# Attention and a routed expert layer: moments kept later, scores waited for by chunk, planning over more tiles, results loaded ahead of z

## What is computed

```
n  = layernorm(x)
q  = relu(n @ Wq + bq); k = relu(ctx @ Wk + bk); v = relu(ctx @ Wv + bv)
x1 = x + relu((relu(q @ k.T) / sqrt(512) + mask) @ v)
z  = layernorm(x1)
topv, topi = top_k(z @ gate_w, 2);  w = softmax(topv)
y_e = (silu(z @ Wu[e]) * (z @ Wv[e])) @ Wo[e]
out = x1 + sum over the two chosen e of w_e * y_e
```

## Time and profile before

| | |
|---|---|
| median of three runs | 429.07 us |
| the profiled execution, span | 429.35 us, 427.6 us |
| TensorE's granted clock, mean | 0.991 of full speed |
| TensorE busy | 404.1 us, 94% |
| VectorE busy | 344.8 us, 81% |
| ScalarE busy | 267.5 us, 63% |
| chain that ended last | TensorE 55%, VectorE 23%, ScalarE 7% |

### The profile page before, as it was taken

The page is one execution under the profiler, slowest core; times in us unless marked ns, Lnnn a source line. Parts: engine busy times, 40 slices in busy tenths (PEclk is TensorE's granted clock), DMA queues, the critical chain, the costliest instruction groups (busy, mean ns, idle before and its releaser), DMA issues.

```text
span 427.6 us, 10469 instructions
## 1 busy us (share of the span) xinstructions
PE 404.1 (94%) x3063; PEld 359.5 (84%) x3063; DVE 344.8 (81%) x1126; ACT 267.5 (63%) x581; POOL 194.5 (45%) x231
## 2 busy tenths in 40 slices
PE   8999999999999999998989889999999998999990
PEld 5698988998889988888778778888999997899970
DVE  2679899999999999999767878778887767888760
ACT  1677877778778777776667656666666443344430
POOL 2011135556655555554546743333333154666641
PEclk9999999999999999999999999999999999999996
DMA  8812235877767677544766868779964689999830
GB/s 288 266 64 70 92 100 202 286 270 255 250 219 240 230 258 260 191 152 159 236 236 194 302 190 278 246 232 304 280 205 104 221 271 366 387 368 400 320 137 36
DMA packets 53622, 97.98 MB, mean 229 GB/s; under 512 B 8384, under 2 KB 19136, under 8 KB 53440
## 3 DMA queue, kind: packets, MB, share of 16 engines
q1 hardware_dynamic: 41648, 63.21, 46.4%
q0 software_dynamic: 11920, 34.10, 21.0%
HBM read 54.15 MB, written 50.80 MB: 245 GB/s over the span
## 4 chain that ended last, share of the span: by engine, by line
PE 55%; DVE 23%; ACT 7%; issue 5%; DMA 3%; SPq 2%; POOL 1%; POOLq 0%; DVEq 0%; ACTq 0%
PE psQ L1531 9%; PE psQ L1532 9%; PE psQ L1533 9%; PE psT L1527 6%; DVE st L1138 4%; DVE x L1127 4%; PE psS L1531 3%; DVE qpT L955 2%; PE psQ L1527 2%; PE psO L1531 2%; PE psZ L1533 2%; PE psZ L1531 2%; PE psO L1532 2%; PE psO L1533 2%; PE psZ L1532 2%
## 5 line engine op out<-in xcount | busy, mean ns | idle before, releaser
L955 DVE TENSOR_TENSOR qT<-psT,qT 128x512 fp32r<-128x512 f32 x103 | 69.4, 688 | 25.5 <-ACT qT L751 25.4
L1531 PE MATMUL psQ<-wuv,qT 128*128 x284 | 86.4, 304 | 0.0
L657 POOL DMA_INDIRECT z_dram<-zb x64 | 70.9, 1108 | 31.3 <-issue 15.3
L1532 PE MATMUL psQ<-wuv,qT 128*128 x284 | 80.2, 283 | 0.0
L1533 PE MATMUL psQ<-wuv,qT 128*128 x284 | 80.1, 282 | 0.0
L1531 PE MATMUL psQ<-qT,wq 128*128 128x256 f32 x256 | 75.1, 294 | 0.0
L1533 PE MATMUL psQ<-qT,wq 128*128 128x256 f32 x256 | 72.4, 283 | 0.0
L1532 PE MATMUL psQ<-qT,wq 128*128 128x256 f32 x256 | 72.4, 283 | 0.0
L751 ACT ACTIVATE qT<-psT 128x512 fp32r<-128x512 f32 x103 | 59.5, 594 | 15.2 <-PE psT L1527 15.2
L1531 PEld LDWEIGHTS psQ<-wuv,qT 128*128 128x128 f32 x284 | 53.7, 189 | 3.0
L1532 PEld LDWEIGHTS psQ<-wuv,qT 128*128 128x128 f32 x284 | 54.0, 190 | 0.0
(11 more groups left out here) (325 smaller groups left out, 1050.5 us busy)
## 6 DMA issues: line engine op xcount, KB each, us to landing
wq<-z_dram SPq DMA_DIRECT2D x42, 264.0 KB, 4.0
xin<-in_x_dram SPq DMA_DIRECT2D x11, 512.0 KB, 4.6
z_dram<-spare SPq DMA_DIRECT2D x17, 264.0 KB, 4.6
qpT<-z_dram SPq DMA_DIRECT2D x17, 264.0 KB, 3.8
acc_dram<-spare SPq DMA_DIRECT2D x17, 256.0 KB, 4.8
...
```

The source lines that it names most:

```text
L657: pool.indirect_dma_start(out=z_dram, out_offset=bass.IndirectOffsetOnAxis(ap=z_of(b)[:, t, ROW_COL + k:ROW_COL + k + 1].bitcast(U32), axi ...
L955: nc.vector.tensor_tensor(o, a, b, ALU.subtract).then_inc(s, 1)
L1531: pe.matmul(o, w[LO], a[HI], start=first, stop=False)
L1532: pe.matmul(o, w[HI], a[LO], start=False, stop=False)
```

## The change

1. `norm_x` leaves VectorE's steps; ScalarE normalises both halves of the next block, one after the other (only the first block keeps it).
2. `keep_stats` moves behind `turned_x`.
3. Scores wait for chunk c's low part ahead of chunk c, not for all four ahead of the first.
4. `turn_logits` is two transposes over the strips; a VectorE reduce (`folded`) adds them into SBUF, and max and max_index read there. The next gate matmuls wait for the reduce. `pick` goes.
5. The plan begins at tile 8 instead of 7 and ends at tile 22 instead of 20; `turn_sched` stands after tiles 10 and 20. `know_pads` moves from tile 7 to 11, and with it SP's copies of the tails go behind `load_z`.
6. From tile 50 on, SP asks for first results ahead of `load_z(t)`, and for 44 and 45 both at tile 50, so that up to tile 56 the results run one ahead of where they were.
7. Two waits are written otherwise and hold the same numbers (15 both times).

```diff
...
@@ -268,7 +268,7 @@
         ps_held = psG[0:1, BT + P:BT + 2 * P]
         ps_key = [psS, psG, psQ[0], psQ[1]]
         ps_log = psG[:, 0:BT]
-        ps_logit = psG[:, BT:BT + TPB * E].rearrange("p (t e) -> p t e", e=E)
+        ps_strips = psG[:, 0:BT].rearrange("p (t c s) -> p t s c", t=TPB, s=STRIP)[:, :, 0:E, :]
         ps_pos = psG[:, BT + 32:BT + 32 + TPB * K * E].rearrange("p (t k e) -> p t k e", k=K, e=E)
         ps_tot = psG[:, BT + 96:BT + 96 + K * E].rearrange("p (k e) -> p k e", e=E)
         psST = [psQ[i][:, 2 * R:2 * R + P] for i in range(2)]
@@ -569,17 +570,12 @@
 
 
             bulk = FIRST_B + RING - 1
-            accs = {bulk - 1: [FIRST_B + LATE, FIRST_B, FIRST_B + 1, FIRST_B + LATE + 1, FIRST_B + LATE + 2]}
-            todo = list(range(FIRST_B + LATE + 3, TILES))
+            todo = [FIRST_B + LATE, *range(FIRST_B, FIRST_B + LATE), *range(FIRST_B + LATE + 1, TILES)]
+            accs = {bulk - 1: [todo.pop(0) for _ in range(5)]}
             for t in range(bulk, TILES):
-                accs[t] = [todo.pop(0) for _ in range(2 if t in (bulk + 4, bulk + 6) else 1)]
+                accs[t] = [todo.pop(0) for _ in range(2 if t in (bulk, bulk + 4) else 1)]
             accs[TILES] = todo
             for t in range(TILES):
-                if EARLY <= t < EARLY + E:
-                    if t == EARLY:
-                        sp.wait_ge(pads_known, 2)
-                        sp.wait_ge(head_stored, 16 * E)
-                    copy_tail(t - EARLY)
                 if FULL + 2 <= t < FULL + 2 + E:
                     fill_acc(t - FULL - 2)
                 if bulk - HELD // 2 <= t < bulk:
@@ -593,10 +589,16 @@
                         sp.wait_ge(res_stored[a % RING], 16 * (rounds(a) + 1))
                     for a in accs[t - 1]:
                         load_acc(a)
-                load_z(t)
                 if t >= bulk:
                     for a in accs[t]:
                         load_acc(a)
+                load_z(t)
+                if EARLY <= t < EARLY + E:
+                    if t == EARLY:
+                        sp.wait_ge(pads_known, 2)
+                        sp.wait_ge(head_stored, 16 * E)
+                    copy_tail(t - EARLY)
+                if t >= bulk:
                     for h in range(HELD):
                         if held_wanted(h) == t:
                             load_held(h)
@@ -769,7 +771,7 @@
 
                 ge(act, nmr1_ready, b.n + 1)
                 nc.scalar.activation(xn[:, t, 0:D], x_of(b)[:, t, :], ACT.Identity, bias=nmr1[:, t:t + 1],
-                                     scale=rstd1[:, t:t + 1]).then_inc(xn1_ready, 1)
+                                     scale=rstd1[:, t:t + 1]).then_inc((xn0_ready, xn1_ready)[t], 1)
 
             def turned_x(b, t):
                 ge(act, xn_turned, 2 * b.n + t + 1)
@@ -877,6 +879,7 @@
                 if not nxt.real:
                     nc.scalar.activation(warm[:, :], minus_half[:, 0:1], ACT.Silu).then_inc(warmed, 1)
                 else:
+                    norm1(nxt, 0)
                     norm1(nxt, 1)
                 queries(2)
                 queries(3)
...
@@ -1172,13 +1173,15 @@
 
                 def values(self):
                     ge(dve, logit_turned, self.b.n + 1)
+                    nc.vector.tensor_reduce(logits[:, :, :], ps_strips, AX.X, ALU.add).then_inc(folded, 1)
+                    ge(dve, folded, self.b.n + 1)
                     for t in range(TPB):
-                        nc.vector.max(top_v[:, t, :], ps_logit[:, t, :]).then_inc(route, 1)
+                        nc.vector.max(top_v[:, t, :], logits[:, t, :]).then_inc(route, 1)
 
                 def indices(self):
                     ge(dve, route, self.n + 2)
                     for t in range(TPB):
-                        nc.vector.max_index(top_i[:, t, :], top_v[:, t, :], ps_logit[:, t, :]).then_inc(route, 1)
+                        nc.vector.max_index(top_i[:, t, :], top_v[:, t, :], logits[:, t, :]).then_inc(route, 1)
 
                 def gaps(self):
                     ge(dve, egap_ready, self.b.n)
@@ -1365,7 +1368,6 @@
                     add_attention(prv, 1)
                 if nxt.real:
                     norm1.shift()
-                    norm_x(nxt)
                 if third.real:
                     put.ranks()
                     put.picked()
@@ -1389,12 +1391,13 @@
                 low(3)
                 if prv.real:
                     norm2.shift()
-                    keep_stats(prv)
                 for t in range(TPB):
                     if nxt.real:
                         turned_x(nxt, t)
                     else:
                         turned_g(t)
+                if prv.real:
+                    keep_stats(prv)
                 if ends_early:
                     plan_ends(0)
                     plan_rows(0)
@@ -1483,35 +1486,37 @@
                     put.rows()
                     put.write()
                     Weigh(last).all()
+                if t == 8:
                     dve.wait_ge(place, PLACE_STEPS * NB)
+                    plan_lengths(1)
+                if t == 9:
+                    plan_ends(1)
+                if t == 10:
+                    plan_rows(1)
+                if t == 11:
+                    keep_sched(1)
                     know_pads()
-                    plan_lengths(1)
-                if t == 8:
-                    plan_ends(1)
-                if t == 9:
-                    plan_rows(1)
-                if t == 10:
-                    keep_sched(1)
                     plan_used(1)
-                if t == 11:
+                if t == 12:
                     lists_sizes()
-                if t == 12:
+                if t == 13:
                     lists_rests()
-                if t == 13:
-                    lists_ends(range(0, 3))
                 if t == 14:
-                    lists_ends(range(3, 5))
                     lists_starts()
                 if t == 15:
+                    lists_ends(range(0, 3))
+                if t == 16:
+                    lists_ends(range(3, 5))
                     lists_skips()
-                if t == 16:
+                if t == 17:
                     lists_rows()
-                if t == 17:
+                if t == 18:
                     lists_heads()
-                if t == 18:
+                if t == 19:
                     lists_cuts()
-                if t == 20:
+                if t == 21:
                     keep_sched(2)
+                if t == 22:
                     keep_kinds()
                 if is_held(t + 1):
                     own_of(t + 1)
@@ -1601,10 +1606,10 @@
 
             def scores(b):
                 g = b.n // NB_G
-                ge(pe, qp_lo, 4 * b.n + 4)
                 if b.n == 0:
                     pe.wait_ge(k_lo, DC)
                 for c in range(DC):
+                    ge(pe, qp_lo, 4 * b.n + c + 1)
                     ins = three(psS[:, 0:BT], [kpT[:, h, c, g * KEYS:(g + 1) * KEYS] for h in range(2)],
                                 [qpT[:, h, c, :] for h in range(2)], c == 0, c == DC - 1)
                 ins.then_inc(s_done, 1)
@@ -1621,6 +1626,7 @@
                 if b.n == 0:
                     pe.wait_ge(w_loaded["small"], 32)
                 ge(pe, zT_ready, 2 * b.n + 2)
+                ge(pe, folded, b.n)
                 ge(pe, place, PLACE_STEPS * (b.n - 1) + 3)
                 for c in range(DC):
                     ins = pe.matmul(ps_log[c * STRIP:(c + 1) * STRIP, :], gw[:, c, :], zT[:, c, :], start=True, stop=True,
@@ -1639,16 +1645,14 @@
 
             def turn_logits(b):
                 ge(pe, logT_ready, b.n + 1)
-                if b.n == 0:
-                    pe.wait_ge(conv_ready, 7)
                 for t in range(TPB):
-                    ins = pe.matmul(ps_logit[:, t, :], logT[:, t * P:(t + 1) * P], pick[:, :], start=True, stop=True)
+                    ins = turn(ps_log[:, t * P:(t + 1) * P], logT[:, t * P:(t + 1) * P])
                 ins.then_inc(logit_turned, 1)
 
             def turn_sched(g):
                 pe.wait_ge(plan, PLANNED[g])
                 if g == 0:
-                    pe.wait_ge(lg_ready, NB - 1)
+                    pe.wait_ge(lg_ready, EARLY_NB + 3)
                 if g == 1:
                     pe.wait_ge(place, PLACE_STEPS * NB)
                 if g > 1:
@@ -1725,7 +1729,7 @@
                     turn_g(1)
                 if old.real:
                     gates(old)
-                if not nxt.real:
+                if b.n == EARLY_NB + 3:
                     pe.wait_ge(sched_ready, 2)
                 scores(b)
                 if old.real:
@@ -1770,9 +1774,9 @@
                     turn_logits(last)
                 if t == 6:
                     ranks(last)
-                if t == 9:
+                if t == 10:
                     turn_sched(1)
-                if t == 19:
+                if t == 20:
                     turn_sched(2)
```

7 lines of the change are left out of this document (3 added, 4 removed).

## The result

The change makes the kernel about 1% slower: five runs took 431.57, 433.84, 434.09, 434.64 and 435.52 us, median 434.09, against 429.07 for five runs of the kernel before. The ratio is 1.0107 (95%: 1.0061 to 1.0153). 427.8 had been forecast, within 424.3 to 431.3, and a time over 433.4 had been given a chance of 0.07. The profiled execution is the shortest of the five, 431.57 us with a span of 429.8, 2.2 us over that of before; the others are 2.3 to 4 us longer still, at a mean granted clock of 0.984 to 0.988 in place of 0.991. So there are two things to find: 2.2 us in the trace, and most of the rest beside it.

A forecast was written before the change was run, and what follows sets the result against it. It took TensorE (busy 94%) and, where it sets the pace, VectorE (81%) as bounds. Terms -1.0 + 0.8 - 0.3 - 1.1 + 2.1 - 1.8 = -1.3 gave 428.05, and 427.8 for the median, range 424.3 to 431.3.

The forecast's parts named there:

- first steps: Attention steps 0 to 2: the bare ScalarE detour delays the turned parts and next projection; +0.8 us (0 to 1.2).
- attention, twelve steady steps: Steps 3 to 14: VectorE's round decides, 0.09 us less a step counted; -1.0 us (-3.0 to +2.4).
- end of the stage: Last attention step: earlier scores -0.5, moved instructions ahead of the low parts +0.2; -0.3 us (-0.7 to +0.2).
- plan, up to tile 23: Plan tiles: links spread over more tiles, tile 7 relieved of 0.9; -1.1 us (-1.6 to -0.4).
- results from tile 48: Tile 46's first result asked for earlier, 0.65 there, about 1.1 from held rows and tiles behind; -1.8 us (-0.6 to -2.6).
- Tile 25's rows: At `turn_g(25)`: schedule written one tile later, rows late, TensorE waits two microseconds; +2.1 us (0.8 to 3.2).
- 0.53 us "before the scores": Attention step: TensorE's wait for low(3) ahead of the scores, said to go with scores by chunk.
- rival 2: Results from tile 48: held rows take the result's place entirely, only 0.6 of 1.8 got; 429.0; chance 0.13.
- Rival 1: low(2) in each step: the ScalarE detour is dearer than its rows say; 432.0; chance 0.2.
- rival 3: Tile 25's rows not late, or little, as the issue follows the schedule faster than 0.90; 425.7; chance 0.1.
- rival 4: Attention steps: VectorE's round falls without the 0.4 us at low(2), 0.3 more a step; 424.0; chance 0.1.

The follow-up runs named there:

- before_again: The kernel before, unedited, run once more for its trace; 428.42 us.
- tails_pool: The changed kernel with the eight copies of tails issued by GpSimd ahead of its stores instead of by SP; ratio 1.0128 to the kernel before.
- plan_only: The kernel before with point 5 alone (plan over more tiles, copies of tails behind `load_z`); ratio 1.0078, +3.3 us.
- after_again: The changed kernel, unedited, run again; ratio 1.0114 to the kernel before in its group.
- attn_only: The kernel before with the attention edits alone (points 1 to 4); ratio 1.0044, +1.9 us.
- after_fixed_2: Second run of the changed kernel with tails ahead of the rows, pads at tile 8, last schedule at tile 20; 428.84 us against 429.47, ratio 0.9986.
- bulk: The kernel before with point 6 alone (the new order of results); ratio 0.9984, -0.7 us.

## Why the prediction was wrong, point by point

The measured column compares the profiled executions of the two kernels, 427.6 and 429.8 us long, by the same marks in both.

| term | forecast | measured | from |
|---|---|---|---|
| start, to nmr of step 0 | none | -0.6 | 25.34 (24.96 in `before_again`) to 24.75 |
| first steps | +0.8 | +0.95 | nmr of step 0 to step 2, 20.85 to 21.80 |
| attention, twelve steady steps | -1.0 | -0.4 | nmr of step 2 to step 14, 142.10 to 141.68 |
| end of the stage | -0.3 | -0.3 | nmr of step 14 to the turn at 211.77, 23.83 to 23.54 |
| plan, up to tile 23 | -1.1 | -0.9 | 66.19 to 65.25 (66.39 in `before_again`) |
| tiles 24 and 25 | +2.1 | +3.9 | three turns, 8.5 to 12.4 |
| results from tile 48 | -1.8 | -0.45 | turn of tile 26 to that of tile 70, 122.26 to 121.81 |
| fall of the clock | none | +1.4 to +1.7 | where it falls, other traces |

The rows but the last add up to the +2.2 us of the two traces. What differs most from the forecast are the tiles 24 and 25 (1.8 more) and the results (1.35 more).

**The step that failed is "Tile 25's rows".** It put SP's load 0.90 us behind the schedule, as before, and asked only when the schedule is written; it came 3.80 behind. The change moves each copy behind its load. The first one, which had been issued at 243.45 while SP waited for the schedule, goes into the row, and the last one is issued at 279.29, behind tile 24's load, and must land before tile 25's load may be asked for. Tile 24's rows, which the forecast put at nothing, were late as well, by 0.92. Together +3.9 in place of +2.1. A moved DMA was noted among the changes and not costed on its queue. That the wait came (2.99, forecast 2.08) looks like a hit and is luck: with the schedule early it stayed. The forecast's own mechanism exists behind it; `tails_pool` shows what it is worth, 1.95.

**The clock** was not among the rivals. A wait of 3 us costs more than its length: 1.35 us in `plan_only`, 1.65 in `after_again`. That would cover more than half of the 2.5 us by which the median exceeds the profiled run, and the mean clocks of these runs (0.984 to 0.988) fit it, but none of them was traced, so it is argued and not shown; the rest is open.

**The steps** went as described in VectorE's queue: low(2) waited, nmr to nmr 11.85. The 0.53 us "before the scores" was misread, as shown above; nothing of the sum for the steady steps hangs on it, since that went by VectorE's round. But 0.09 a step was a difference of larger pieces, and 0.01 to 0.04 came: the time freed by `norm_x` was eaten by ScalarE, as forecast, and what moments and chunks gave (0.16, for which 0.27 had been put) was eaten by the fold (0.17 to 0.24). The fold's price from the earlier trace rows (0.25) was near. The Trainium skill's ("VectorE: DVE Perf Modes", TRN2 errata) quicker start from SBUF does not show, as MAX8 takes 0.24 from psG in the kernel before and 0.24 from the folded logits.

**The attention edits in time**: +1.9 us alone (1.0023 to 1.0066), where the stage itself is only 0.2 longer in the trace. In the profiled run of `attn_only` the rest lies behind tile 45, at a result that came late (2.26 us of wait, 0.60 in `before_again`), far from any edit; whether it comes with the edits isn't settled. `after_fixed_2` doesn't speak against it: +1.9 with the -0.7 of the results and the -1.1 of the plan would be 1.0002, inside its interval. What is shown is the split: the fold and the detour together cost what the other two points give.

**The results** are the second term that was mis-sized. The wait of 1.68 went and the held row's of 1.03 stands where forecast. But the 1.1 put on the held rows and the tiles behind did not come: VectorE's waits for results behind tile 45 add up to 3.13 us before and 2.85 after, and the kernel before alone differs by 0.6 between its two traces (3.13 and 2.52). They move more than they shrink. By time `bulk` gives -0.7 (-1.5 to +0.2), which excludes the 1.8 of the forecast and agrees with rival 2's 0.6 and with no change alike.

**The plan and the rivals.** The plan's gain came near the forecast, though the parts listed for it don't add up to it: -0.9 + 0.15 - 0.2 - 0.4 + 2 x 0.25 is -0.85, and the -1.1 counts the fold once. Rival 1 (432.0) was near in time for the wrong reason, as low(2) waited less (0.29) than the forecast itself had put; rival 3 is wrong; rival 4's 0.3 a step was seen only in another order on ScalarE.

The landing of the loads was 2.7 to 3.2 us from 276 to 285 us, shorter than the 3.4 of the earlier trace rows. The Trainium skill's fit ("DMA: Bandwidth & Descriptors", anatomy of one DMA), which it gives for DMAs issued by GpSimd and not by SP, makes an estimate of 2.6 for their size, nearer here than in the kernel before. It changed little, since the issue was late.
